# A decoder layer's third phase: values by four full-width products in k's bank, k in one product, attended rows tile by tile

## Chip, core, metric

One NeuronCore of a Trainium2 chip computes the layer. The time is the device time of one execution in microseconds. TensorE multiplies matrices, VectorE, ScalarE and GpSimd work element by element, SyncE starts transfers. TensorE writes its results to PSUM, eight banks of 512 columns of 32-bit numbers in each of 128 partitions; the other engines read them there.

## What is computed

128 sequences of 64 tokens with 128 features pass through linear attention with a lookup activation, then cross attention to a context, then a small mixture of experts, each followed by a layer norm. The change lies in the cross attention, of which the reference keeps this:

```python
q = (x @ WQ).reshape(b, s, H, DK).transpose(0, 2, 1, 3)          # H = 16 heads, DK = 8
k = (encoder_output @ WK).reshape(b, s, H, DK).transpose(0, 2, 1, 3)
v = (encoder_output @ WV).reshape(b, s, H, DK).transpose(0, 2, 1, 3)
scores = jnp.where(m != 0, NEG, jnp.einsum('bhqd,bhkd->bhqk', q, k) / SQRT_DK)
ctx = jnp.einsum('bhqk,bhkd->bqhd', jax.nn.softmax(scores, axis=-1), v).reshape(b, s, d)
return ctx @ WO
```

All matrices are 32-bit numbers. The profile shows each such product as two records.

## The kernel before

Tokens are worked on in tiles of 128, two sequences each, and four tiles form a group; there are 16 groups (NG) and 64 tiles (NT). Phase 1 is the linear attention and phase 2 the lookup activation; both run over groups. Phase 3, from about 255 us to the end, holds cross attention and experts. It is a software pipeline written out by hand: every engine has a function `phase3(s, p)` that lists, in its own order, what it does in stage s, in four slots t = 0 to 3, one for each tile n = 4s + t. Stage s works on scores, softmax and weighing of group s, on the projections of group s + 1, on output product and norm of group s - 1 and on the experts of groups s - 1 and s - 2. Engines meet only in semaphores: `wait_ge` waits for a count, `then_inc` adds to it, and an engine's instructions run in order, so that all behind a wait wait with it. The loops are unrolled, and the order of an engine's work is the order of the text.

TensorE's slot: turn the probabilities of tile n (`turn_probabilities`, L1437), one or two small jobs, open the scores of two later tiles (`scores_open`, L1419, slots 0 and 2), weigh the values of tile n (`weigh_values`, L1449), close the scores (`scores_close`, L1430). Its small jobs are `turn_y` and the four expert products of earlier groups in slot 0, the output product `rows_product(bank(6), attT, w_xo)` (L1244) and q's product (`project_qk`, L1485) in slot 1, the values' product (`project_v`, L1495) in slot 2, three expert products (`moe`, L1507) in slot 3. The product of k for the next group (`project_k_half`, L1487) is in two halves of 256 columns, one in front of the close of slot 0 and one behind it, in bank 5. The close of slot 0 waits for `max_ready`: VectorE must first have taken maxima of the opened half of the scores (`opened_maxima`, L1056).

`project_v` makes 16 products: for each of 8 sequences u and each half h of the features, 64 tokens are the weights and 64 columns of `w_xv` the moving operand, so that even heads land in partitions 0 to 63 and odd heads in 64 to 127 of bank 4. `copy_v` (L786) on ScalarE takes bank 4 into `v2` with two copies of 64 partitions and 512 columns. Bank 4 is also that of y's transposes and of q; k, and two of the expert products, use bank 5 (`MOE_BANK`, L45).

`weigh_values` puts even tiles into the first 144 columns of bank 7 and odd tiles into the next 144. VectorE's `xattend` (L1042) divides the rows of two tiles at once by their sums, a reciprocal (L1048) and a product (L1050): tiles 0 and 1 at the end of slot 1, tiles 2 and 3 in slot 3. Only in the last stage are tiles 2 and 3 taken one by one. VectorE's order in a stage (L1161): small maxima of the experts' gate, opened maxima, shift of tile 2 (L1072, L1089), residual with the output product (L1146) and its statistics, shift of tile 3 (L1076, L1082), `xattend` of tiles 0 and 1, the gate's weights, the mask of the next group (L1157), shift of the next group's tile 0, `xattend` of tiles 2 and 3, shift of its tile 1, last statistics.

## Time and profile before

| | |
|---|---|
| Median of 3 runs | 550.61 us (549.78 to 551.66) |
| The profiled execution, its own time | 552.82 us |
| Its span | 551.1 us |
| TensorE, products | 500.5 us busy, 91% |
| TensorE, weight loads | 375.0 us, 68%, beside the products |
| VectorE | 399.5 us, 72% |
| GpSimd | 373.1 us, 68% |
| ScalarE | 351.3 us, 64% |
| Mean TensorE clock granted | 0.984 of full speed |

Busy shares are means over three phases and say little of one edit. For that, one stage is read in the timeline, row by row: when each instruction starts, how long it runs, and, where its engine stood idle before it, for how long and what released it. A wait for several semaphores is put down to the one that the profile saw last. The ends of products are modelled. "Issue" as a releaser means that the engine waited for nothing that the profile shows.

### The profile page before, as it was taken

The page shows a single profiled execution, that of the slowest core. Times are in us where ns is not written, and L with a number is a line of the kernel's source. Part 1 is how long each engine was busy: PE and PEld are TensorE (multiplying, and loading weights), DVE is VectorE, ACT ScalarE, POOL GpSimd, SP SyncE. Part 2 cuts the span into 40 slices and gives each one's busy share as a digit, 9 for nine tenths or more (in the row PEclk, how much of TensorE's full clock was granted, in tenths as well). Part 3 has the DMA queues.
Part 4 walks back from the last instruction along what each step waited for, and adds up shares of the span by engine and source line. Part 5 has one row for each costly group of instructions (what it writes and reads, how often), then busy time and mean ns, then how long its engine had stood idle before and what let it go on. Part 6 is the DMA issues. An engine that isn't in the chain of part 4 may idle for free. (4 is left out here: it accounts for less than half of the span.)

```text
span 551.1 us, 23040 instructions
## 1 busy us (share of the span) xinstructions
PE 500.5 (91%) x9358; PEld 375.0 (68%) x9358; DVE 399.5 (72%) x1356; ACT 351.3 (64%) x637; POOL 373.1 (68%) x684
## 2 busy tenths in 40 slices
PE   3899999998999999999899999989999999999780
PEld 1677777775777777676667776767767677767570
DVE  3777777765677667756568788878778788887866
ACT  2566666656777777764576677757666677766641
POOL 3666666645668774746156878897878778797734
PEclk9999999999999999999899999999999999999977
DMA  6540000000000000010110210221101110110001
GB/s 169 157 133 2 3 2 1 4 2 1 2 0 2 2 1 1 2 30 3 32 32 4 51 44 12 52 51 51 32 24 51 52 39 24 44 51 23 23 2 58
DMA packets 24747, 17.44 MB, mean 32 GB/s; under 512 B 2113, under 2 KB 22465, under 8 KB 24641
## 3 DMA queue, kind: packets, MB, share of 16 engines
q1 hardware_dynamic: 24208, 15.90, 10.6%
q8 instruction: 74, 1.21, 0.9%
q14 instruction: 33, 0.26, 0.2%
q10 hardware_dynamic: 432, 0.07, 0.1%
HBM read 11.77 MB, written 4.19 MB: 29 GB/s over the span
## 5 line engine op out<-in xcount | busy, mean ns | idle before, releaser
L810 ACT ACTIVATE soft<-pair 128x1024 f32<-128x1024 f32 x64 | 51.9, 810 | 50.1 <-PE pair L1445 49.5
L803 ACT ACTIVATE soft<-soft,row_scale 128x512 f32<-128x512 f32 x96 | 66.2, 721 | 15.4 <-DVE soft L1089 10.4
L1387 PEld LDWEIGHTS pair<-w,gel 128*128 128x128 f32 x512 | 60.5, 192 | 8.2 <-issue 5.9
L1387 PE MATMUL pair<-w,gel 128*128 128x128 f32 x512 | 62.7, 276 | 1.0 <-ACT gel L736 1.0
L1348 PE MATMUL pair<-hT,w 128*128 128x512 f32 x128 | 58.3, 595 | 1.3 <-ACT lev L731 1.3
L553 POOL TENSOR_SCALAR k_exp<-k_sb,quad_mask 128x512 f32<-128x512 f32 x64 | 43.2, 693 | 20.1 <-ACT k_sb L783 10.6
L1445 PE MATMUL pair<-ident,soft 128*128 128x128 f32 x384 | 55.6, 281 | 1.3 <-ACT soft L803 1.3
L1076 DVE TENSOR_REDUCE neg_max<-pair 128x16 f32<-128x512 f32 (+1 forms) x48 | 41.1, 856 | 14.5 <-PE pair L1412 14.4
L1445 PEld LDWEIGHTS pair<-ident,soft 128*128 128x128 f32 x384 | 43.3, 141 | 12.0 <-issue 6.4
L515 POOL TENSOR_TENSOR X<-X,proj_sb 128x512 f32<-128x512 f32 x16 | 20.4, 1274 | 35.3 <-ACT proj_sb L694 35.3
L1412 PE MATMUL pair<-k_exp,qT 32*32 32x128 f32 (+1 forms) x2048 | 43.5, 336 | 0.0
L1089 DVE TENSOR_TENSOR soft<-pair,neg_max 128x512 f32<-128x512 f32 x64 | 41.2, 686 | 1.1
L1348 PEld LDWEIGHTS pair<-hT,w 128*128 128x128 f32 x128 | 22.9, 190 | 24.0 <-issue 23.5
L1239 PE MATMUL pair<-ident,xn 128*128 128x128 f32 x192 | 30.6, 283 | 8.6 <-DVE xn L361 8.6
L321 POOL TENSOR_SCALAR veps_b<-mv_b 128x4 f32<-128x4 f32 (+1 forms) x33 | 7.8, 236 | 44.4 <-DVE mv_b L312 25.8
L736 ACT ACTIVATE gel<-lev 128x512 f32<-128x512 int8 x64 | 36.4, 621 | 0.9 <-DVE lev L985 0.9
L1239 PEld LDWEIGHTS pair<-ident,xn 128*128 128x128 f32 x192 | 23.7, 146 | 18.5 <-issue 15.8
L323 POOL TENSOR_TENSOR rstd_b<-veps_b,minus_half 128x4 f32<-128x4 f32 (+1 forms) x33 | 34.4, 1042 | 2.8
L323 POOL TENSOR_TENSOR rstd<-veps,minus_half 128x4 f32<-128x4 f32 x32 | 33.2, 1039 | 2.7
L1476 PEld LDWEIGHTS pair<-v,soft 128*32 128x32 f32 x2048 | 23.6, 109 | 14.7 <-issue 14.7
L1244 PE MATMUL pair<-w_kv,hT 128*128 128x128 f32 x256 | 33.5, 285 | 0.0
L305 DVE BATCH_NORM_STATS2 stats_b<-X 128x6 f32<-128x128 f32 x128 | 28.0, 281 | 5.7 <-DVE X L1146 2.8
(145 smaller groups left out, 1260.1 us busy)
## 6 DMA issues: line engine op xcount, KB each, us to landing
X<-in_x SPq DMA_DIRECT2D x16, 256.0 KB, 3.2
cT<-in_ctx SPq DMA_DIRECT2D x16, 256.0 KB, 3.9
out_rows<-X SPq DMA_DIRECT2D x15, 256.0 KB, 2.6
mask_rows<-in_mask_early SPq DMA_DIRECT2D x16, 128.0 KB, 3.9
w<-in_L_attn_w SPq DMA_DIRECT2D x2, 256.0 KB, 3.3
out_rows<-X SPq DMA_DIRECT2D x2, 128.0 KB, 1.8
w_kv<-in_L_attn_wk SPq DMA_DIRECT2D x1, 64.0 KB, 2.9
w_kv<-in_L_attn_wv SPq DMA_DIRECT2D x1, 64.0 KB, 2.6
```

The lines of the kernel that those rows point to most:

```text
L323: nc.gpsimd.tensor_tensor(rstd[:, ts], veps[:, ts], minus_half[:, ts], ALU.pow)\
L553: last = nc.gpsimd.tensor_scalar(k_exp[q][:, h, :], k_sb[:, :], quad_mask[:, h:h + 1], 0.0, ALU.mult, ALU.add)
L736: nc.scalar.activation(gel[:, p, f, :], lev[f][:, :], ACT.Gelu_apprx_tanh, scale=QSTEP).then_inc(gel_ready, 1)
L803: nc.scalar.activation(part, part, ACT.Exp, scale=row_scale[:, n:n + 1])\
L810: nc.scalar.activation(pT[par].rearrange("p (a c) -> p a c", a=2), turned, ACT.Copy)\
L1076: nc.vector.tensor_reduce(neg_max[par][:, :].rearrange("p (a h) -> p a h", a=2), scores, AX.X, ALU.max, negate=True).then_inc(max_ready, 1)
L1089: nc.vector.tensor_tensor(rows[:, heads, :], scores[:, half, :, :], neg_max[par][:, heads].unsqueeze(2).broadcast_to([P, HH, S]), ALU.add) ...
L1239: last = nc.tensor.transpose(dst[:, P * t:P * (t + 1)], src[:, t, :], ident[:, :])
L1348: nc.tensor.matmul(bank(up_bank(s, f)), w_1[:, P * f:P * (f + 1)], hT[p][:, :], start=True, stop=True).then_inc(up_done, 1)
L1387: last = nc.tensor.matmul(bank(6 + q)[:, P * t:P * (t + 1)], gel[:, q, f, P * t:P * (t + 1)], w_2[:, f, :], start=(f == 0), stop=(f == NF ...
L1412: last = nc.tensor.matmul(pair[t % 2][b * QW:(b + 1) * QW, quad // 2, heads], qT[p][rows, batch + first:batch + first + QW], k_exp[p][rows ...
L1445: last = nc.tensor.transpose(dst, probability_rows(n)[:, P * i:P * (i + 1)], ident[:, :])
```

## The change

Four things are done. `project_v` makes four products, one for each tile u, of 128 tokens as weights and all 128 columns of `w_xv`, in bank 5 (bank 1 for group 0, as before). Even and odd heads then lie beside each other, and the two sequences of a tile in the two halves of the partitions, so that `copy_v` sorts them with four copies of 64 partitions and 256 columns: sequence b, head parity h. The product of k is made in one piece of 512 columns behind the close of slot 0. `weigh_values` puts every tile into the same 144 columns of bank 7 and waits in each tile until the tile before was attended, and `xattend` takes one tile at a time: tile 0 in slot 0 behind the opened maxima, tile 1 where the pair was, tile 2 in slot 2 behind the next mask, tile 3 in slot 3. Waits follow the banks: `turn_y` waits for the copy of q and no longer for that of the values, the values' product waits for the copy of k, the first expert product for the copy of the values and the third for that of q.

```diff
--- before.py
+++ after.py
@@ -786,12 +786,13 @@
             def copy_v(g, q):
                 after(act, pv_done, g * TG - TG)
                 act.wait_ge(xv_done, g + 1)
-                for h in range(2):
-                    rows = slice(h * S, (h + 1) * S)
-                    last = nc.scalar.activation(
-                        v2[q][rows, :, :, h, 0:DH],
-                        bank(first_bank(g, 4))[rows, :].rearrange("p (b i e) -> p b i e", i=HH, e=DH),
-                        ACT.Copy)
+                values = bank(first_bank(g, 5)).rearrange("p (u h i e) -> p u h i e", u=TG, h=2, e=DH)
+                for b in range(2):
+                    for h in range(2):
+                        batches = v2[q][h * S:(h + 1) * S, :, :, h, 0:DH] \
+                            .rearrange("p (u b) i e -> p u b i e", b=2)
+                        last = nc.scalar.activation(batches[:, :, b, :, :],
+                                                    values[b * S:(b + 1) * S, :, h, :, :], ACT.Copy)
                 last.then_inc(v2_ready, 1)
 
             def probabilities(n):
@@ -1039,19 +1040,16 @@
                     ln_statistics(dve, ln_a, r, lambda t: X[:, r * TG + t, :], stats_b, mv_b,
                                   ln_a.offs, r * 2)
 
-            def xattend(n, p, part):
+            def xattend(n, p, t):
 
                 dve.wait_ge(pv_done, n + 1)
-                count = len(part)
-                src = bank(7)[:, H * HV * (part[0] % 2):H * HV * (part[-1] % 2 + 1)] \
-                    .rearrange("p (h e) -> p h e", e=HV)
-                nc.vector.reciprocal(rec[:, 0, 0:H * count], src[:, :, DH]).then_inc(xrec_ready, count)
+                src = bank(7)[:, 0:H * HV].rearrange("p (h e) -> p h e", e=HV)
+                nc.vector.reciprocal(rec[:, 0, 0:H], src[:, :, DH]).then_inc(xrec_ready, 1)
                 dve.wait_ge(xrec_ready, n + 1)
-                nc.vector.tensor_tensor(
-                    att[p][:, part[0]:part[-1] + 1, :].rearrange("p t (h e) -> p (t h) e", e=DH),
-                    src[:, :, 0:DH],
-                    rec[:, 0, 0:H * count].unsqueeze(2).broadcast_to([P, H * count, DH]),
-                    ALU.mult).then_inc(xatt_ready, count)
+                nc.vector.tensor_tensor(att[p][:, t, :].rearrange("p (h e) -> p h e", e=DH),
+                                        src[:, :, 0:DH],
+                                        rec[:, 0, 0:H].unsqueeze(2).broadcast_to([P, H, DH]),
+                                        ALU.mult).then_inc(xatt_ready, 1)
 
             def opened_maxima(n):
 
@@ -1166,26 +1164,27 @@
                         gate_top(old, p)
                     if t == 0 and exists(s):
                         opened_maxima(n + 2)
+                        after(dve, xatt_xposed, s - 1)
+                        xattend(n, p, t)
                     if t == 1 and exists(s):
                         shift(n + 1, 0)
                     if t == 1 and exists(prev):
                         residual(prev, 6, range(TG))
                     if t == 1 and exists(s):
                         shift(n + 2, 1)
-                        after(dve, xatt_xposed, s - 1)
-                        xattend(n, p, (0, 1))
+                        xattend(n, p, t)
                     if t == 1 and exists(old):
                         gate_weights(old)
                     if t == 2 and exists(s + 1):
                         future_keys(s + 1, q)
-                    if t == 2 and s == LAST:
-                        xattend(n, p, (2,))
+                    if t == 2 and exists(s):
+                        xattend(n, p, t)
                     if t == 3 and exists(s + 1):
                         shift(n + 1, 0)
                     if s == LAST and t == 3:
                         residual(*halves[0][:1], 5, halves[0][1])
                     if t == 3 and exists(s):
-                        xattend(n, p, (3,) if s == LAST else (2, 3))
+                        xattend(n, p, t)
                     if t == 3 and exists(s + 1) and s >= 0:
                         shift(n + 2, 1)
                     if t == 3 and exists(old) and s < LAST:
@@ -1449,23 +1448,20 @@
             def weigh_values(n, t, p):
 
                 pe.wait_ge(pT_ready, n + 1)
-                if n % 2 == 0 or n == NT - 1:
-                    after(pe, xatt_ready, n)
-                first = H * HV * (n % 2)
+                after(pe, xatt_ready, n)
                 if n % 2:
                     pe.wait_ge(v4_ready, (n // TG + 1) * QB)
                     pe.wait_ge(future_ready, n // TG + 1)
                     for b in range(QB):
                         nc.tensor.matmul(
-                            bank(7)[b * QW:(b + 1) * QW, first:first + H * HV],
+                            bank(7)[b * QW:(b + 1) * QW, 0:H * HV],
                             future[p][:, t // 2, b * QW:(b + 1) * QW],
                             v2[p][:, t // 2 * QB + b, :, :, :].rearrange("p i h e -> p (i h e)"),
                             start=True, stop=False)
                     for i in range(QB):
                         for b in range(QB):
                             last = nc.tensor.matmul(
-                                bank(7)[b * QW:(b + 1) * QW,
-                                        first + QB * HV * i:first + QB * HV * (i + 1)],
+                                bank(7)[b * QW:(b + 1) * QW, QB * HV * i:QB * HV * (i + 1)],
                                 pT[1][:, P * i + b * QW:P * i + (b + 1) * QW],
                                 v4[p][:, t // 2 * QB + b, i, :, :].rearrange("p h e -> p (h e)"),
                                 start=False, stop=i == QB - 1)
@@ -1484,10 +1480,6 @@
 
                 nc.tensor.matmul(dst, w[:, :], src[:, :], start=True, stop=True).then_inc(done, 1)
 
-            def project_k_half(q, half):
-                cols = slice(GW // 2 * half, GW // 2 * (half + 1))
-                return nc.tensor.matmul(bank(5)[:, cols], w_xk[:, :], cT[q][:, cols], start=True, stop=True)
-
             def turn_y(g):
                 pe.wait_ge(ln_a.done, g + 1)
                 transposes(X[:, tiles(g), :], bank(first_bank(g, 4)), y_xposed)
@@ -1495,13 +1487,9 @@
             def project_v(g, q):
 
 
-                for u in range(2 * TG):
-                    for h in range(2):
-                        last = nc.tensor.matmul(bank(first_bank(g, 4))[h * S:(h + 1) * S,
-                                                                       FH * u:FH * (u + 1)],
-                                                cT[q][:, S * u:S * (u + 1)],
-                                                w_xv[:, FH * h:FH * (h + 1)],
-                                                start=True, stop=True)
+                for u in range(TG):
+                    last = nc.tensor.matmul(bank(first_bank(g, 5))[:, P * u:P * (u + 1)],
+                                            cT[q][:, P * u:P * (u + 1)], w_xv[:, :], start=True, stop=True)
                 last.then_inc(xv_done, 1)
 
             def moe(g, t):
@@ -1537,7 +1525,7 @@
                         turn_attended(q, 6, range(TG))
                     if t == 0 and exists(g):
                         after(pe, moe_ready, (s - 1) * TG - 1)
-                        after(pe, v2_ready, g)
+                        after(pe, q_ready, g)
                         turn_y(g)
                     if t == 1 and exists(r):
                         pe.wait_ge(xattT_ready, r + 1)
@@ -1546,7 +1534,7 @@
                         pe.wait_ge(yT_ready, g + 1)
                         project_qk(yT, w_xq, bank(4), xq_done)
                     if t == 2 and exists(g):
-                        pe.wait_ge(q_ready, g + 1)
+                        pe.wait_ge(k_ready, g + 1)
                         project_v(g, q)
                     if t == 2 and s == LAST:
                         pe.wait_ge(xatt_ready, n)
@@ -1565,22 +1553,20 @@
                         if n == 0:
                             pe.wait_ge(ysum_ready, NG)
                         weigh_values(n, t, p)
+                    if exists(s) and t % 2 == 0 and n + 2 < NT:
+                        scores_close(n + 2, n + 3)
                     if t == 0 and exists(g):
                         pe.wait_ge(ctx_loaded[q], (g - q) * 8 + 16)
                         after(pe, moe_ready, s * TG - TG)
                         after(pe, k_ready, g)
-                        project_k_half(q, 0)
-                    if exists(s) and t % 2 == 0 and n + 2 < NT:
-                        scores_close(n + 2, n + 3)
-                    if t == 0 and exists(g):
-                        project_k_half(q, 1).then_inc(xk_done, 1)
+                        project_qk(cT[q], w_xk, bank(5), xk_done)
                     if t == 3 and exists(r) and s < LAST:
                         pe.wait_ge(y2T_ready, r + 1)
                         if exists(g):
-                            pe.wait_ge(k_ready, g + 1)
+                            pe.wait_ge(v2_ready, g + 1)
                         for u in range(TG - 1):
                             if u == 2 and exists(g):
-                                pe.wait_ge(v2_ready, g + 1)
+                                pe.wait_ge(q_ready, g + 1)
                             moe(r, u)
```

## Rows read from the trace of the kernel before

**Rows 1.** Windows, phase 3 by stage: us, engines' busy us (records), clock, DMA, GB/s

```profile
289.61:306.71 17.10, 16.52 (x451) 12.28 (x443) 14.07 (x45) 12.01 (x24) 11.70 (x20) 1.00 0.02 4
...
sum 227.29, PE 216.33 PEld 159.67 DVE 182.87 ACT 156.31 POOL 183.35; mean PE 16.64 PEld 12.28 DVE 14.07 ACT 12.02 POOL 14.10
```

**Rows 2.** Timeline, slot 0: start us, us, engine line op out<-in, [idle before <-releaser]

```profile
411.03 0.82 PE L1476 MATMUL pair<-v,soft 128*32 128x18 f32 x64
...
411.35 0.69 DVE L1059 TENSOR_REDUCE neg_max<-pair 128x8 f32<-128x512 f32 x1
...
411.78 0.70 PE L1489 MATMUL pair<-cT,w_xk 128*128 128x256 f32 x2
...
412.41 0.28 PE L1401 MATMUL pair<-causal_bf,quad_ident 32*128 32x256 bf16 x4
...
413.22 0.70 PE L1489 MATMUL pair<-cT,w_xk 128*128 128x256 f32 x2
...
413.53 0.69 DVE L1072 TENSOR_REDUCE neg_max<-pair 128x8 f32<-128x512 f32 x1 [1.49 <-PE pair L1412]
...
413.75 0.60 PE L1445 MATMUL pair<-ident,soft 128*128 128x128 f32 x4
```

**Rows 3.** Timeline, slot 1 of that stage, and the same place 71.8 us earlier

```profile
414.19 1.06 PE L1244 MATMUL pair<-w_xo,attT 128*128 128x128 f32 x8
...
415.08 1.02 PE L1485 MATMUL pair<-yT,w_xq 128*128 128x512 f32 x2
...
415.46 0.68 DVE L1146 TENSOR_TENSOR X<-X,pair 128x512 f32<-128x512 f32 x1
...
416.04 0.45 PE L1459 MATMUL pair<-v,future 128*32 128x144 f32 x8
...
343.74 1.06 PE L1244 MATMUL pair<-w_xo,attT 128*128 128x128 f32 x8
...
344.84 0.69 DVE L1146 TENSOR_TENSOR X<-X,pair 128x512 f32<-128x512 f32 x1
```

**Rows 4.** Timeline, end of VectorE's chain and slot 2 of that stage

```profile
417.74 1.15 PE L1500 MATMUL pair<-w_xv,cT 128*64 128x64 f32 x32
...
418.43 0.69 DVE L1082 TENSOR_TENSOR soft<-pair,neg_max 128x512 f32<-128x512 f32 x1
...
419.22 0.28 PE L1401 MATMUL pair<-causal_bf,quad_ident 32*128 32x256 bf16 x4 [0.33 <-ACT soft L810]
```

**Rows 5.** Timeline, attended rows of two tiles, the weighing and the next shift

```profile
419.04 0.35 DVE L1048 RECIPROCAL rec<-pair 128x32 f32<-128x32 f32 x1
...
419.49 0.42 DVE L1050 TENSOR_TENSOR att<-pair,rec 128x256 f32<-128x256 f32 x1
...
420.06 0.79 PE L1476 MATMUL pair<-v,soft 128*32 128x18 f32 x64
...
421.89 1.23 DVE L1076 TENSOR_REDUCE neg_max<-pair 128x16 f32<-128x1024 f32 x1 [0.28 <-PE pair L1412]
```

**Rows 6.** Timeline, the last stage: its second scores, attended rows of one tile

```profile
516.92 0.28 PE L1401 MATMUL pair<-causal_bf,quad_ident 32*128 32x256 bf16 x4 [0.39 <-DVE neg_max L1059]
...
524.48 0.69 PE L1521 MATMUL pair<-ident,att 128*128 128x128 f32 x2 [2.95 <-DVE att L1050]
...
526.30 0.26 DVE L1048 RECIPROCAL rec<-pair 128x16 f32<-128x16 f32 x1 [0.76 <-PE pair L1476]
...
526.59 0.29 DVE L1050 TENSOR_TENSOR att<-pair,rec 128x128 f32<-128x128 f32 x1
```

**Rows 7.** Timeline of ScalarE: copies of the values, of tile 3, of 256 columns

```profile
419.78 1.26 ACT L791 ACTIVATE v<-pair 64x512 f32<-64x512 f32 x2
...
422.27 0.60 ACT L810 ACTIVATE soft<-pair 128x512 f32<-128x512 f32 x1 [1.23 <-PE pair L1445]
...
525.21 0.39 ACT L827 ACTIVATE attT<-pair 128x256 f32<-128x256 f32 x1 [0.82 <-PE pair L1521]
```

**Rows 8.** Timeline, inside a weighing of values

```profile
368.23 0.24 PE L1476 MATMUL pair<-v,soft 128*32 128x18 f32 x4 [0.94 <-issue]
```

## The prediction

> **What bounds the kernel now.** I read the windows of the decoder's third phase first (the tail of the span from about 255 us on, where everything that the diff touches runs, save the values of group 0). Thirteen full stages, measured from one product of k to the next, take 227.29 us together, 17.5 each; one of the shortest takes 17.10, with TensorE busy 16.52 us in it and 16.64 on the mean [rows 1]. So TensorE is almost always at work, and a stage is 17.1 us plus something irregular. The other engines are at 12 to 14 us of 17.1. That does not say yet that a saving on TensorE is a saving in time: for that the timeline of one stage has to be read for who releases whom.
>
> TensorE's order in a stage has three places where it meets VectorE. At slot 0 it weighs values (411.03), multiplies the first half of k (411.78) and closes the scores (412.41), which must wait for VectorE's early maxima, 411.35 to 412.04 [rows 2]. At slot 1 VectorE takes the scores at 413.53, runs without idle time through the shift of tile 2, the residual at 415.46, the statistics and the shift of tile 3, which ends at 419.12 [rows 2 to 4]. At slot 2 TensorE is done with the values at about 418.9, sits 0.33 us and opens scores at 419.22 [rows 4]. The profile puts that wait down to ScalarE's copy, but the subtraction on VectorE ended at 419.12, 0.10 before, so I take VectorE as the one waited for. From the close of slot 0 to the open of slot 2 the stage is therefore set by VectorE: 419.22 - 413.22 = 6.00 us, and TensorE has 0.33 us to spare there.
>
> **Values by four products.** Thirty-two records of 64 columns took 1.15 us (two records for each of 16 products) [rows 4]. The nearest row for four products of 128 columns with 128 columns of weights is the output product, eight records, 1.06 us, and 0.89 to the start of the next [rows 3]. So 0.1 to 0.25 us less TensorE time, but in a place where TensorE then waits 0.33 us for VectorE: worth nothing in the 15 stages of phase 3, and -0.1 once, for group 0, whose values are multiplied in phase 2 where no such wait follows. The new wait on the copy of k is free: k ended at 413.92, a copy of 128x512 takes 0.60 us, and the values start only at 417.74 [rows 2, 4, 7].
>
> **Four copies for two.** ScalarE took 1.26 us for two of 64x512 [rows 7]. The nearest row for 256 columns is 0.39 us [rows 7], so four take 1.3 (pipelined like the two) to 1.6 us, 0.0 to 0.3 more, at 419.8 to 421.4 instead of 421.04. ScalarE's next work, turned probabilities of tile 3, starts only at 422.27 [rows 7]. Cover of 0.9 us: nothing. The expert products now wait for this copy one product earlier, at about 424, also covered.
>
> **k in one piece after the close.** Before: first half 0.63 us (411.78 to 412.41), second half 0.53 (413.22 to 413.75), 1.16 in all [rows 2]. One product of 512 columns, the one for q, takes 416.04 - 415.08 = 0.96 from its start to the next product [rows 3]. TensorE saves 0.20. But the first half also hid the wait for the maxima. Without it the close waits for VectorE: 412.04 plus the step from VectorE to TensorE, which the last stage shows, since it has no k: there TensorE idles 0.39 us at this very place, released by the maxima [rows 6]. So close moves from 412.41 to about 412.19: 0.22 earlier, with 0.41 of idle time in front. Counted from there: all of k follows, 0.96 instead of 0.53, so the output product starts 0.96 + 0.44 = 1.40 after the close instead of 0.97, and ends 1.06 later, at +2.46. VectorE needs it for the residual. It reaches the residual 415.46 - 413.22 = 2.24 after the close today, and the product ended at 415.25 (2.03), 0.21 ahead. In another stage the product ended at 343.74 + 1.06 = 344.80 and the residual began at 344.84: this is the case where it is waited for, and the step is 0.04 [rows 3]. New: 2.46 + 0.04 = 2.50, that is 0.26 late. Against the 0.22 gained at the close: +0.04 at most, I take +0.02 a stage (the close may come a little earlier still), 15 stages, **+0.3**. TensorE itself gets to the open of slot 2 at +0.96 instead of +0.53 and less the shorter values, 0.2 to 0.3 later than before against the close, and has 0.33: it just fits.
>
> **Attended rows tile by tile.** Each pair costs VectorE 0.80 us (419.04 to the next at about 419.84) [rows 5]; single tiles exist in the last stage, 526.30 to 526.88, 0.58 [rows 6]. Four for two: +0.72 us of VectorE a stage. Where do they lie? Tile 0 goes in front of the shift of tile 2, where VectorE waited 1.4 us; it can start when the values of slot 0 are done, about 412.1, and ends by 412.7, before the scores arrive at 413.3: covered by 0.6. Tile 2 goes in front of the next group's first shift, where VectorE waited 0.28 us [rows 5]; the chain before it is 0.21 shorter, together 0.49 against 0.58: that shift comes 0.1 later. What hangs on it is TensorE's turn of the first probabilities, behind ScalarE's exponentials; the cover there is about 0.2 to 0.3, so 0. At slot 3 the chain is 0.21 shorter again and the delay is made good before the early maxima. TensorE's new waits, one in front of every weighing, are for rows that are done 0.9 us (tile 2), over 2 us (tile 0) before. One is on the path and gets better: at slot 2 TensorE opens scores until about 420.03, and the pair's rows end at 419.91, so that the weighing at 420.06 waits for them by some 0.03 [rows 4, 5]. With one tile they end 0.21 earlier: -0.03 x 15 = **-0.4**. In the last stage TensorE waits 2.95 us for just these rows before it turns them [rows 6]; one tile for two ends that 0.21 earlier: **-0.2**.
>
> **Fewer instructions.** 24 products and their weight loads in two records each for the values, one for k: 48 + 4 = 52 of about 894 records a stage. The stages' irregular part is 227.29 - 13 x 17.10 = 5.0 us. Part of it shows as idle time inside a run of equal products that wait on no semaphore, put down to issue: 0.94 us in front of the last 4 of 64 [rows 8]; there are four such rows in the phase, all at this place. It looks like the sequencer running out of instructions: 64 products and as many loads start within 0.75 us there [rows 2], right behind the stretch that the change thins out. Bounds: 0 (the stalls only move), -5.0 (all gone), and +3 (they fall in worse places, as often as now and as long as the longest). I take an eighth, **-0.6**.
> The Trainium skill ("Runtime: NRT & Kernel Launch", Instruction fetch mechanics) states that instructions are refilled in blocks of 256 while the current block runs, and that this fetch is hidden. By that rule the last term is nothing and the result would be 550.2; the idle time inside a run without semaphores speaks against the rule, though no row shows the fetch that is waited for.
>
> **The sum.** -0.1 + 0.3 - 0.4 - 0.2 - 0.6 = -1.0 us against the profiled execution's 552.82 (span 551.1), 551.8. That execution was 2.2 us above the median of the runs, 550.61, so 549.6.
>
> **The rivals.**
> First, the early close is kept. If the output product does not hold the residual (its record's end is modelled, and the step of 0.04 may be too long), VectorE's 6.00 us start 0.22 earlier and the open of slot 2 follows: -0.22 x 15 = -3.3 where the sum has +0.3, 549.6 - 3.6 = 546.0. For it: VectorE is the bound between the two places. Against: the stage in which residual and product meet at 0.04. I give it 0.13.
> Second, the stalls go: -3 to -5 instead of -0.6, 545.2 to 547.2, the middle 546.2. For it: they lie in the densest stretch, right behind the values. Against: most stages with the same code show nothing there. 0.15.
> Third, slower: the close of slot 0 has lost its cover. Today the maxima may come up to 0.23 late unseen; afterwards every delay of VectorE passes to TensorE, and from there back into VectorE's own chain. The place is 411.35: VectorE ends its small maxima just then and the scores arrive just then. If the added rows of tile 2, or of tile 0 in front of the shift, put VectorE 0.2 late (instead of 0.1 early), each stage grows by 0.2 and the residual's 0.04: +3.4 with the other terms, 553.0. It decides from the point where tile 2's rows delay the next shift by more than the 0.21 given back at slot 3. With stalls that fall in worse places it is of the same size. 0.20.
> Fourth, a V whose products are not shorter, or copies that take 1.6 us: both are covered, the time stays in the forecast's range.
>
> **How the numbers follow.** Forecast 0.52, own range 548.4 to 550.9; first 0.13, second 0.15, third 0.20. A measurement of this kernel can tell about 0.3%, 1.65 us: faster is below 548.96, slower above 552.26. Faster: the first two and 0.09 of the forecast, 0.37. Slower: most of the third, 0.18 (its small end is within). Same: 0.45. The range reaches from the middle of the second rival to the third: 546.0 to 552.9.
>
> **What would show it.** Right: in front of the close of slot 0 idle time of about 0.4 us on TensorE, released by the early maxima, in all stages; the residual waits for the output product by about 0.25; the wait at the open of slot 2 is still there, 0.1 to 0.3; V about 0.9 to 1.0 us; shortest stage 17.05 to 17.15. Rival one: residual without a wait, shortest stage 16.9. Rival two: shortest stage the same, but all near it. Rival three: the idle time at the close above 0.5, or the weighing of slot 3 or 1 behind rows. Wrong altogether: a wait in front of a place that I called covered.

## The result and the profile after

The kernel with the change takes **553.87 us** (median of 13 runs, 552.59 to 556.40); the kernel before, in the same comparison, 551.23 (13 runs, 548.91 to 552.75). The ratio is **1.0047 [1.0025, 1.0069]**: slower by 2.6 us. The prediction was 549.6, with a range of 546.0 to 552.9; the median lies 1.0 above its top. It set out from a median of 550.61 for before, which 13 runs put at 551.23: 0.6 of the 4.3 us between forecast and result come from there.

| | before | after |
|---|---|---|
| Median | 551.23 us | 553.87 us |
| The profiled execution, its own time | 552.82 us | 552.99 us |
| Its span | 551.1 us | 551.2 us |
| TensorE, products | 500.5 us | 494.9 us |
| VectorE | 399.5 us | 407.2 us |
| ScalarE | 351.3 us | 354.9 us |
| Instructions, all engines | 23040 | 22289 |
| Clock granted | 0.984 | 0.984 |

One thing has to be kept in mind for all that follows: the two profiled executions differ by 0.17 us only, because that of before was 1.6 us above its median and that of after 0.9 below. The traces show what the schedule became and where irregular time falls. How much of it an execution has on the mean, only the medians tell.

Four stages of the kernel after, windows from one product of q to the next; columns as in [rows 1]:

```profile
293.64:310.76 17.12, 16.19 (x418) 11.93 (x417) 14.50 (x49) 12.27 (x25) 14.28 (x26) 1.00 0.02 5
380.30:399.03 18.73, 16.61 (x418) 12.05 (x417) 14.59 (x49) 12.28 (x25) 14.24 (x26) 1.00 0.13 38
399.03:416.16 17.13, 16.20 (x419) 12.01 (x418) 14.50 (x49) 12.28 (x25) 14.28 (x26) 1.00 0.14 43
433.28:451.56 18.28, 16.36 (x418) 11.97 (x417) 14.71 (x49) 12.33 (x25) 14.21 (x26) 1.00 0.18 49
```

A clean stage takes 17.12 to 17.13 us where it took 17.10 [rows 1], with 0.33 us less of TensorE work in it. VectorE has four more instructions and 0.43 us more work. Stages of 18 us and more are still there. (A clean stage is one without a stall, at the full clock. A window's record counts take in records that reach over its ends; the program has 442 product records in a stage of before and 416 in one of after.)

The clean stage that begins at 399.03, TensorE's timeline (start us, us, engine line op out<-in, [idle before <-releaser]), to be read against [rows 2 to 5]:

```profile
411.91 0.82 PE L1472 MATMUL pair<-v,soft 128*32 128x18 f32 x64
413.06 0.28 PE L1400 MATMUL pair<-causal_bf,quad_ident 32*128 32x256 bf16 x4 [0.33 <-DVE neg_max L1057]
...
413.86 1.13 PE L1481 MATMUL pair<-cT,w_xk 128*128 128x512 f32 x2
414.83 0.60 PE L1444 MATMUL pair<-ident,soft 128*128 128x128 f32 x4
415.26 1.06 PE L1243 MATMUL pair<-w_xo,attT 128*128 128x128 f32 x8
...
418.72 1.06 PE L1491 MATMUL pair<-w_xv,cT 128*128 128x128 f32 x8
420.13 0.28 PE L1400 MATMUL pair<-causal_bf,quad_ident 32*128 32x256 bf16 x4 [0.35 <-ACT soft L811]
```

The same stage, VectorE's timeline:

```profile
412.22 0.69 DVE L1057 TENSOR_REDUCE neg_max<-pair 128x8 f32<-128x512 f32 x1 [0.30 <-PE pair L1411]
412.86 0.26 DVE L1047 RECIPROCAL rec<-pair 128x16 f32<-128x16 f32 x1
...
414.18 0.69 DVE L1070 TENSOR_REDUCE neg_max<-pair 128x8 f32<-128x512 f32 x1 [0.74 <-PE pair L1411]
...
416.36 0.69 DVE L1144 TENSOR_TENSOR X<-X,pair 128x512 f32<-128x512 f32 x1 [0.17 <-PE pair L1243]
...
419.34 0.69 DVE L1080 TENSOR_TENSOR soft<-pair,neg_max 128x512 f32<-128x512 f32 x1
```

TensorE's waits over the whole trace of after (waited for: us in total, times, longest), and its turn of the attended rows in the last stage, which stood 2.95 us behind them in [rows 6]:

```profile
PE pair L1400 <- DVE neg_max L1057: 5.3, 16, 0.4
```
```profile
524.40 0.69 PE L1509 MATMUL pair<-ident,att 128*128 128x128 f32 x2 [2.64 <-DVE att L1049]
```

The schedule came out as predicted, stage by stage. In front of the close of slot 0 TensorE idles 0.33 us, released by the maxima, in all 16 stages. k follows in one piece, 0.97 us to the next product. The output product ends at 415.26 + 1.06 = 416.32 and holds the residual, which starts at 416.36 after 0.17 us of idle time (0.25 predicted); in the waits of the whole trace VectorE's residual is held by this product 16 times, before only twice. V takes 1.06 us for 1.15 and a wait of 0.35 is still behind it. The places that were called covered show no new wait.

What is left is the idle time put down to issue, in the middle of runs of equal products. In after's trace:

```profile
264.65 0.41 PE L1411 MATMUL pair<-k_exp,qT 32*32 32x128 f32 x4 [0.75 <-issue]
...
384.27 0.28 PE L1400 MATMUL pair<-causal_bf,quad_ident 32*128 32x256 bf16 x4 [0.35 <-ACT soft L811]
384.48 0.66 PE L1411 MATMUL pair<-k_exp,qT 32*32 32x256 f32 x32
385.07 0.82 PE L1472 MATMUL pair<-v,soft 128*32 128x18 f32 x64
385.83 0.28 PE L1400 MATMUL pair<-causal_bf,quad_ident 32*128 32x256 bf16 x4
386.04 0.66 PE L1411 MATMUL pair<-k_exp,qT 32*32 32x256 f32 x24
387.89 0.42 PE L1411 MATMUL pair<-k_exp,qT 32*32 32x128 f32 x8 [1.19 <-issue]
...
441.15 0.27 PE L1444 MATMUL pair<-ident,soft 128*128 128x128 f32 x1 [0.99 <-issue]
457.39 0.28 PE L1400 MATMUL pair<-causal_bf,quad_ident 32*128 32x256 bf16 x4 [0.24 <-issue]
```

Before, four such rows stood at one place, in front of the last 4 of 64 records of slot 2's weighing [rows 8], together 2.66 us. Two more, which the prediction did not count, stand inside the weighing of an odd tile:

```profile
284.00 0.41 PE L1466 MATMUL pair<-v,soft 128*32 128x36 f32 x25 [0.22 <-issue]
...
423.73 0.41 PE L1466 MATMUL pair<-v,soft 128*32 128x36 f32 x25 [0.29 <-issue]
```

Now each of the four is at another place: in front of the last 8 or 4 of 32 records of slot 2's close, just behind that close, in front of a close. Together the stalls are 3.17 us in either trace.

### The profile page after: what moved, and what is told of

It reads as the page before. It is cut to its first block and busy times, and to the rows that moved or that the text cites. A ratio compares the mean times of both kernels' runs of the same rounds, so it can differ in the third digit from the quotient of the medians.

```text
span 551.2 us, 22289 instructions
## 1 busy us (share of the span) xinstructions
PE 494.9 (90%) x8944; PEld 370.3 (67%) x8944; DVE 407.2 (74%) x1418; ACT 354.9 (64%) x669; POOL 372.0 (67%) x684
## 3 DMA queue, kind: packets, MB, share of 16 engines
q8 instruction: 71, 1.16, 0.9%
## 5 line engine op out<-in xcount | busy, mean ns | idle before, releaser
L1411 PE MATMUL pair<-k_exp,qT 32*32 32x128 f32 (+1 forms) x2048 | 44.8, 333 | 1.9 <-issue 1.9
L305 DVE BATCH_NORM_STATS2 stats<-X 128x6 f32<-128x128 f32 x128 | 27.6, 278 | 5.4 <-DMA X<-in_x 4.0
```

Of the source, the lines that this page charges most:

```text
L305: last = nc.vector.bn_stats(stats[:, t, :], rows(t))
L1411: last = nc.tensor.matmul(pair[t % 2][b * QW:(b + 1) * QW, quad // 2, heads], qT[p][rows, batch + first:batch + first + QW], k_exp[p][rows ...
```

## Theories

**A, the instruction blocks.** Count TensorE's instructions in the program: each product record and each load record is one, so a 32-bit product is four and a bf16 product or a transpose two, and each wait that stands as an instruction of its own is one more. The stalls put down to issue in phase 3 then lie at one position of a raster of 256 instructions: counted from the start of the kernel's TensorE program, 84 stalls in the 14 traces of this case stand at position 190 or 191 of 256. (Another 14 idle stretches put down to issue, of 0.16 to 0.24 us, do not: 13 in before_wandering and one in k_one_piece_filled. They lie in front of the open of slot 2 behind tiny products, where TensorE waited for VectorE before.) The stall at 387.89 shows a whole block: the 256 instructions in front of it are 2 x (4 + 32 + 64 + 4 + 24) = 256, that is everything from the open at 384.27 on. The profile's queue of instructions moved 1.16 MB in 71 packets, 16 KB each, and 74 packets in before, whose program has some 800 instructions more. So TensorE's instructions come in blocks, and where a block has been worked off faster than the next one is ready, TensorE waits at the block's end. A stage of before has 896 instructions (442 products, 442 loads, 12 waits), and two stages are exactly 7 blocks: block ends fall in the same places again and again. A stage of after has 846 (48 fewer for V, 4 fewer for k, 2 more waits), and the block ends wander through all places, also those behind the densest instructions.

**B, the schedule.** The time is lost by the edits themselves: k in one piece takes the cover from the close, or V and its copies hold something in executions that the trace didn't catch.

The Trainium skill ("Runtime: NRT & Kernel Launch", Instruction fetch mechanics) gives blocks of 256 instructions, refilled while the current one runs; with that these traces agree. It calls the cost of crossing a block's end "mostly hidden": from 255 us on, 668 block ends in the 14 traces pass without a stall and 84 do not, with 0.16 to 1.76 us each.

## The experiments

**1. The block ends moved, nothing else (pad128_before).** Before, with waits that are already fulfilled ahead of TensorE's first work:

```diff
+            for _ in range(128):
+                pe.wait_ge(const_ready, 1)
             pe.wait_ge(w1_loaded, PHASE1_WEIGHTS)
```

> The kernel before, with 128 extra waits on a count long reached at the very start of TensorE's program, where TensorE is idle anyway. Nothing of the schedule changes; all later TensorE instructions lie half a 256-instruction block further on. Theory A (the change lost time because instructions are refilled in blocks, and the kernel before, whose two stages take exactly seven blocks, had block ends at harmless places): the time moves by 1 us or more from the 551.2 of before, more likely up, to 552 to 554. Theory B (the loss is in the changed schedule itself): within 0.5 us of before, once a later start of the first product is taken off.

Measured: 563.2 us (560.76 to 569.01), ratio **1.0227 [1.0184, 1.027]**. That is far above the 552 to 554 that theory A expected. Of the loss, some 2 us are the waits themselves (the first product comes 2.3 us later); 10 us are not. (The profiled execution, 569.01, is the slowest of the six.) Two waits share an instruction, so the shift was 64, not 128. Two stages in windows, then TensorE's timeline in the second:

```profile
297.70:314.80 17.10, 16.53 (x445) 12.30 (x444) 14.06 (x45) 12.00 (x24) 14.28 (x26) 1.00 0.01 4
314.80:334.80 20.00, 18.45 (x445) 13.49 (x444) 14.30 (x45) 12.50 (x24) 14.23 (x26) 0.91 0.16 41
```
```profile
319.02 0.28 PE L1403 MATMUL pair<-causal_bf,quad_ident 32*128 32x256 bf16 x4 [0.33 <-ACT soft L810]
...
320.79 0.66 PE L1414 MATMUL pair<-k_exp,qT 32*32 32x256 f32 x24
322.67 0.42 PE L1414 MATMUL pair<-k_exp,qT 32*32 32x128 f32 x8 [1.22 <-issue]
...
324.42 0.71 PE L1461 MATMUL pair<-v,future 128*32 128x144 f32 x8
...
325.53 2.31 PE L1510 MATMUL pair<-w_moe,y2T 128*128 128x263 f32 x6
```

The place moved from the last 4 records of the weighing to the last 8 of 32 of the close behind it: 2 x (4 + 4 + 24) = 64 instructions on, and since two stages are 7 blocks, block ends of two neighbouring stages lie 128 apart, so that 64 back and 64 on is the same. The clean stage is untouched, 17.10. Each second stage takes 19.9 to 20.4, the last 18.35. The waits of 0.84 to 1.50 us at this place are 7 in phase 3 (8.6 us in the summary of waits), and behind all but the shortest the clock falls: the granted clock is 0.50, the lower of its two levels, from 323.6 to 327.0 and 1.00 again afterwards, and six records of expert products take 2.31 us at 325.53 where they take 1.60 in an undisturbed stage. In before, the block that ends in the last 4 records of the weighing holds V, the open and 60 records:

```profile
399.77 1.15 PE L1500 MATMUL pair<-w_xv,cT 128*64 128x64 f32 x32
...
403.51 0.24 PE L1476 MATMUL pair<-v,soft 128*32 128x18 f32 x4 [0.66 <-issue]
```

What a stall waits for can be read from the packets of the instruction queue in the traces. In all 14, from 255 us on, there is one packet for each block end. Some ends of blocks (us; "lag" is from the end of the packet to TensorE's first product behind the block's end):

| trace | block begins | its packet | next block begins | stall | lag |
|---|---|---|---|---|---|
| before | 295.58 | 295.40 to 296.52 | 298.46 | none | 1.94 |
| before | 329.95 | 330.43 to 331.33 | 332.83 | none | 1.50 |
| before | 364.23 | 366.05 to 367.02 | 368.23 | 0.94 | 1.21 |
| before | 399.78 | 401.16 to 402.14 | 403.51 | 0.66 | 1.37 |
| pad128_before | 319.02 | 320.11 to 321.47 | 322.67 | 1.22 | 1.20 |
| after | 384.28 | 385.35 to 386.61 | 387.89 | 1.19 | 1.28 |
| after | 411.33 | 411.23 to 412.15 | 413.55 | none | 1.40 |
| shift128_before | 454.23 | 456.62 to 457.59 | 459.05 | 1.76 | 1.47 |

All 84 stalls end 1.19 to 1.61 us (median 1.38) after the block's packet, and at none of the 668 ends without a stall is it shorter than 1.19. So TensorE waits for the next block's instructions. How long depends on two things: how fast the block is worked off, and when its packet starts, which is 0.25 to 4.0 us after the block's beginning where there is a stall. The same block of before (V, the open, 60 records) passes at 298.46 and 332.83 and stalls at 368.23 and 403.51, because its packet started later. This is theory A; theory B has no edit here to act on.

**2 to 4. Each part of the change alone**, in one comparison with run 1.

> The kernel before with k's product in one piece behind the close of slot 0, and nothing else. Theory B puts the loss here: the close waits about 0.4 us for the maxima and the output product holds the residual, 0.04 to 0.17 us a stage, 551.8 to 553.8. Theory A: 4 instructions fewer a stage let the block ends drift slowly, 550.5 to 553.5 with the stalls at other places than before; the shortest stage 17.10 to 17.15.

> The kernel before with the attended rows taken tile by tile in one place of bank 7, and nothing else. TensorE's instructions are the same but for one wait in front of every odd weighing. Both theories expect little: shortest stage 17.05 to 17.10, 550.5 to 551.5. If VectorE's 0.72 us more a stage were what costs, 552 to 554 with TensorE waiting in front of a weighing or of the close.

> The kernel before with the values by four products in k's bank and four copies, and nothing else. 48 instructions a stage fewer. Theory B: covered, 551.0 to 551.3. Theory A: this part carries the loss, since it alone makes the block ends drift through the stage: 552.5 to 554, with a shortest stage of 17.10 as before and stalls put down to issue at places that differ from stage to stage.

```diff
 k_one_piece
-                        project_k_half(q, 0)
                     if exists(s) and t % 2 == 0 and n + 2 < NT:
                         scores_close(n + 2, n + 3)
-                        project_k_half(q, 1).then_inc(xk_done, 1)
+                        project_qk(cT[q], w_xk, bank(5), xk_done)
 rows_one_tile: xattend(n, p, t) for each tile, as in the change
 v_four_products: project_v and copy_v of the change, in bank 5
```

| | instructions a stage | ratio | clean stage |
|---|---|---|---|
| before | 896 | 1 | 17.10 |
| k_one_piece | 892 | 1.0066 [1.0044, 1.0089] | 17.12 to 17.13 |
| rows_one_tile | 898 | 0.9986 [0.9968, 1.0004] | 17.09 |
| v_four_products | 848 | 1.0077 [1.0048, 1.0105] | 17.04 to 17.10 |

k_one_piece (554.18) and v_four_products (555.50) lie above what either theory expected, 553.8 and 554 at most; rows_one_tile (550.43) is just below the expected 550.5. The parts do not add up: +3.6, -0.8 and +4.2 us are 7.0 where the change costs 2.6. V alone makes the clean stage no longer and is the slowest of all; theory B has no place for that. rows_one_tile has two instructions more than before, both waits, and its block end walks back by two records in every second stage:

```profile
368.16 0.30 PE L1471 MATMUL pair<-v,soft 128*32 128x18 f32 x11 [0.63 <-issue]
...
403.18 0.31 PE L1471 MATMUL pair<-v,soft 128*32 128x18 f32 x13 [0.66 <-issue]
...
437.92 0.32 PE L1471 MATMUL pair<-v,soft 128*32 128x18 f32 x15 [0.37 <-issue]
...
472.65 0.32 PE L1471 MATMUL pair<-v,soft 128*32 128x18 f32 x17 [0.39 <-issue]
```

Two instructions a stage are four in two stages, the length of two products with their loads: 11, 13, 15, 17. That is the raster, read off a timeline.

**5 to 7. Other shifts.** Tiny products of two columns into columns of bank 7 that nothing uses, ahead of TensorE's first work, four instructions each:

```diff
+            pe.wait_ge(const_ready, 1)
+            def filler(count):
+                for _ in range(count):
+                    nc.tensor.matmul(bank(7)[0:QW, 500:502], ident[0:QW, 0:QW], ident[0:QW, 0:2],
+                                     start=True, stop=True)
+            filler(32)    # 28 in shift112_before; 42 in shift168_after
```

> The kernel before with 32 tiny products (128 TensorE instructions) ahead of its first one, in TensorE's idle start. Since two stages take exactly 7 blocks of 256 instructions, a shift by half a block only makes odd and even stages change places. Theory A (time is lost where a block ends inside dense instructions, and how much depends on the place): the same as before, 550.5 to 552, against 563.2 for the shift by 64. If a filled start as such costs time, or a shift as such: 555 or more. Shortest stage 17.1 under either.

> The same with a shift by 112. Theory A, from the places at which blocks end (a block is never worked off in less than about 3.65 us, the dense ones would take 2.1 to 3.4): block ends move 16 instructions further down, out of the close of slot 0's end, summed shortfall 7.9 us instead of 10.5 and none above 1 us in a stage: 548.5 to 551. Theory B (the place does not matter below the one bad case): 551.2 as before.

> The changed kernel with a shift by 168 instructions in the idle start. Its stages take 846 instructions, so that block ends wander through the stage and no shift avoids the dense places; with this one two ends instead of four fall where the shortfall is above 1 us. Theory A: 550 to 552.5, 1.5 to 4 us less than the 553.9 of the changed kernel. Theory B (the changed schedule costs the time): 553.5 to 554.5, unchanged.

Measured: shift128_before 554.98 us, 1.0051 [1.0027, 1.0076], and shift112_before 554.11 us, 1.0039 [1.0015, 1.0064]: both slower than theory A expected. shift168_after 551.99 us, 1.0013 [0.999, 1.0035], is where theory A had it, but this shows little alone: the same comparison's before is 552.36, and the interval meets that of after, 1.0025 to 1.0069. The shift by 128 puts the stalls where they were, in front of the last 4 of 64, as expected, but they are longer:

```profile
352.39 0.24 PE L1483 MATMUL pair<-v,soft 128*32 128x18 f32 x4 [1.21 <-issue]
...
459.05 0.24 PE L1483 MATMUL pair<-v,soft 128*32 128x18 f32 x4 [1.76 <-issue]
```

So the place says where TensorE may wait, not how long. At this place the packet starts 1.10 to 2.39 us after the block's beginning in the six stalls of shift128_before, and 2.39 in front of the 1.76; before it is -0.17 to 1.82. Nor is there a shortest time for a block, which the expectation of shift112_before put at 3.65 us: the one of after at 411.33 passes in 2.22 us without a stall, since its packet was early. Shifts that differ by little can't be ranked by place alone.

**8. The stage of after filled up to 896 (after_full_stage)**, with 50 instructions, 12 tiny products and one small transpose, ahead of the close of slot 0 and ahead of V (and 13 tiny products at the start, not shown):

```diff
+                        filler(6, 5)     # ahead of the close of slot 0: 24 instructions
 ...
+                        filler(6, 5)     # ahead of V, with the transpose: 26 instructions
+                        nc.tensor.transpose(bank(5)[0:QW, 304:304 + QW], ident[0:QW, 0:QW], ident[0:QW, 0:QW])
```

> The changed kernel with its 50 missing instructions a stage put back as tiny products where TensorE waits for VectorE anyway (26 ahead of the values' product, 24 ahead of the close of slot 0), and 52 at the start, so that stages take 896 instructions again and blocks end at the same places of the weighing of slot 2 as in the kernel before. Schedule and waits are those of the changed kernel. Theory A: 550 to 551.5, the loss against before gone. Theory B: 553.5 to 555.

Measured: 562.57 us, 1.0196 [1.0161, 1.0231], where 550 to 551.5 was expected. The fillers themselves cost time: on one place of 32 columns they are not short (12 records, 0.47 us to the next product), and seven of the eight stalls stand in the close behind them.

```profile
418.97 0.54 PE L1237 MATMUL pair<-ident 32*32 32x2 f32 x12
...
421.26 0.42 PE L1418 MATMUL pair<-k_exp,qT 32*32 32x128 f32 x9 [0.95 <-issue]
```

The clean stage was 17.56, 0.44 longer than that of after, 6.6 us in 15 stages. Nothing follows for the change.

**9 to 11. The number of instructions alone.** Fillers spread over the four column groups, in each stage ahead of V only, into columns that V then overwrites or nothing reads (after_filled has 13 more at the start, not shown):

```diff
+                for i in range(count):
+                    rows = slice(i % QB * QW, (i % QB + 1) * QW)
+                    nc.tensor.matmul(bank(b)[rows, 500:502], ident[:, rows], ident[:, 0:2],
+                                     start=True, stop=True)
 ...
+                        filler(12, 5)   # after_filled: 846 + 48 + 2 (the small transpose of run 8) = 896
+                        filler(1, 4)    # k_one_piece_filled: 892 + 4 = 896
+                        filler(3, 4)    # before_wandering: 896 + 12 = 908
                         project_v(g, q)
```

> The changed kernel with its 50 missing instructions a stage put back as 12 tiny products and one small transpose ahead of the values' product, spread over four column groups so that they take about 0.3 us and fit into the wait for VectorE at the open of slot 2, and 52 at the start. Stages take 896 instructions again, and blocks end at the same places of the weighings as in the kernel before (3 instructions off). Theory A (place of block ends): the loss goes, ratio to before 0.998 to 1.001 instead of 1.0047, shortest stage 17.12. Theory B (the changed schedule costs the time): 1.004 to 1.006. If the filling itself does not fit, the shortest stage shows it, above 17.2.

> k in one piece as in the run with that part alone (ratio 1.0066), plus one tiny product (4 instructions) a stage ahead of the values' product: 896 instructions a stage again, block ends at the same places of the weighings as before. Theory A: ratio 0.999 to 1.002. Theory B: 1.006 to 1.007, since one more product cannot make it faster.

> The kernel before with three tiny products (12 instructions) a stage ahead of the values' product, where TensorE has 0.33 us to spare; nothing else. Stages take 908 instructions, so that block ends wander as they do in the changed kernel. Theory A: three stages get a shortfall of 1.2 to 1.5 us and the slow clock with it, ratio 1.003 to 1.009, shortest stage 17.1. Theory B: ratio 1.000 to 1.001.

| | instructions a stage | ratio | clean stage |
|---|---|---|---|
| after | 846 | 1.0047 [1.0025, 1.0069] | 17.12 |
| after_filled | 896 | 1.0013 [0.9997, 1.0029] | 17.32 to 17.33 |
| k_one_piece | 892 | 1.0066 [1.0044, 1.0089] | 17.12 |
| k_one_piece_filled | 896 | 1.0017 [1.0001, 1.0032] | 17.12 |
| before_wandering | 908 | 1.0081 [1.0056, 1.0107] | 17.09 |

Each ratio is to the before of its own comparison; the two filled kernels and before_wandering share one. This settles it. Four instructions in a stage, one tiny product, take k_one_piece from +3.6 us to +0.9, with the same schedule. Twelve instructions more in before, which leave its clean stage at 17.09, cost 4.1 us on the median (555.07 against 550.96). And after with 50 more instructions, which lengthen each clean stage by 0.2 us, 3 us in all (the filling was expected to fit, at 17.12), is still faster than without them, 1.0013 against 1.0047, though the two intervals touch. In k_one_piece_filled the stalls are back at one place, in before_wandering they are anywhere:

```profile
401.99 0.24 PE L1482 MATMUL pair<-v,soft 128*32 128x18 f32 x4 [0.77 <-issue]
...
437.46 0.24 PE L1482 MATMUL pair<-v,soft 128*32 128x18 f32 x4 [0.74 <-issue]
...
473.12 0.24 PE L1482 MATMUL pair<-v,soft 128*32 128x18 f32 x4 [0.75 <-issue]
```
```profile
316.49 0.66 PE L1451 MATMUL pair<-ident,soft 128*128 128x128 f32 x4 [0.95 <-issue]
...
351.63 0.44 PE L1418 MATMUL pair<-k_exp,qT 32*32 32x128 f32 x12 [0.89 <-issue]
...
456.80 0.31 PE L1482 MATMUL pair<-v,soft 128*32 128x18 f32 x12 [0.92 <-issue]
```

The stalls at block ends in phase 3 add up to 3.17 us in before, 2.84 in k_one_piece_filled, 5.55 in before_wandering, 6.49 in shift128_before, 9.78 in pad128_before, and 0.85 in after_filled (the two rows below). But each is one execution, and small differences do not follow the medians: k_one_piece has 2.39 and v_four_products 3.68, and the profiled execution of k_one_piece is only 0.4 us above that of before, where the medians are 3.2 apart. The longest stall of before_wandering is 0.95 us, not the expected 1.2 to 1.5, and the clock falls behind one.

```profile
402.98 0.25 PE L1479 MATMUL pair<-v,soft 128*32 128x18 f32 x6 [0.55 <-issue]
...
434.75 0.37 PE L1239 MATMUL pair<-ident 128*32 128x2 f32 x24
...
438.13 0.25 PE L1479 MATMUL pair<-v,soft 128*32 128x18 f32 x6 [0.30 <-issue]
```

**12. A version meant to beat both (reordered).** k_one_piece_filled, with the output product and k moved to the head of slot 1, y's transposes moved between the weighing and the close of slot 0, VectorE's opened maxima ahead of the gate's small ones, and ScalarE's copy of y behind the exponentials of tile 1. Of TensorE's part:

```diff
+                    if t == 1 and exists(r):
+                        rows_product(bank(6), attT, w_xo[:, :]).then_inc(xproj_done, 1)
+                    if t == 1 and exists(g):
 ...
+                        project_qk(cT[q], w_xk, bank(5), xk_done)
                     if exists(s):
                         turn_probabilities(n, t)
```

> A version meant to beat both, built on the kernel before: y's transposes take the place of k's first half ahead of the close of slot 0, the output product and then all of k come right behind that close, VectorE takes the opened maxima before the gate's small maxima, ScalarE copies y after the exponentials of tile 1, and one tiny product a stage keeps 896 instructions. The wait of 0.33 us at the open of slot 2 is used up by k. Expected: shortest stage 16.75 to 16.9 instead of 17.1, 546 to 549 in all, less what block ends at new places cost (up to +3).

Measured: 551.6 us, 1.001 [0.9994, 1.0025], where 546 to 549 was expected. The shortest stage is 17.14. At slot 0 the copy of the turned probabilities is now waited for, since y's transposes no longer cover it, and from the output product (413.17) to the open of slot 2 (419.40) TensorE needs 6.23 us without a wait, more than the 6.00 of VectorE that the move was to shorten:

```profile
410.22 0.28 PE L1407 MATMUL pair<-causal_bf,quad_ident 32*128 32x256 bf16 x4 [0.23 <-ACT soft L810]
...
413.17 1.16 PE L1250 MATMUL pair<-w_xo,attT 128*128 128x128 f32 x8
...
419.40 0.28 PE L1407 MATMUL pair<-causal_bf,quad_ident 32*128 32x256 bf16 x4
```

No kernel here beats before by more than can be told; rows_one_tile, 0.9986 [0.9968, 1.0004], comes nearest.

## Why the prediction was wrong

**What bounds the kernel**: right. VectorE from the close of slot 0 to the open of slot 2, TensorE everywhere else; the wait at that open stayed, 0.35 for 0.33.

**V and its copies**: right. 1.06 us against the 1.15 of before, nothing gained in the stages, since the wait behind it takes it in; no wait for the copies. For group 0 the values take 0.89 us to the next product where they took 1.08, but the first scores of the phase open at 240.75 as they did at 240.69: the 0.1 does not show. V alone left the clean stage at 17.04 to 17.10.

**k in one piece**: right in each step. Idle 0.33 for about 0.4 at the close; the residual held by the output product and starting 0.04 behind its end; +0.02 a stage predicted, and k_one_piece's clean stage is 0.02 to 0.03 longer. With the block ends left in place (k_one_piece_filled) it costs 0.9 us, with an interval from 0.1 to 1.8; 0.3 was predicted.

**Attended rows**: right. Predicted -0.4 and -0.2; the wait in the last stage went from 2.95 to 2.64, and the part alone gave -0.8, with an interval that takes in 0.

**The first rival** did not happen (the residual waits), **nor the second**, as far as the change goes: the stalls did not go, they add up to the same 3.17 us in the trace. Its neighbour, stalls that go where the stage stays at 896 and V's block is filled, is after_filled. **The third** gave the right side and nearly the size, 553.0, by luck, since its mechanism is not what happened: the opened maxima wait 0.30 us for TensorE at 412.22, so VectorE isn't late there. What came true is the sentence beside it, stalls that fall in worse places.

**The step that failed is the term "Fewer instructions".** It took the stalls for a sequencer that runs dry behind dense stretches, asked how much its neighbourhood thins out, and put -0.6 between -5.0 and +3. What the runs showed in its place: the stalls stand at the ends of blocks of 256 instructions, the number of instructions in a stage decides where these ends fall, and this term is most of the +2.6 us. It should have asked where the stalls come from. The evidence was in [rows 8]: four stalls in front of the same 4 of 64 records, in four successive second stages, which points to something periodic that two stages' length happens to be a multiple of. (The prediction read these as all there are; the two others, in the odd weighing, stand at the same position of the blocks.) The count of 52 of about 894 records came near the program's 50 of 896 instructions, and 896 is 3.5 times 256: that gives the raster, and with it that the change breaks it. Then the bound +3 is the likely value: the schedule's terms (+0.3 to +0.5 for 15 clean stages, -0.3 in the last stage) come to about nothing. The size by itself is shown for k: +3.6 us with 892 instructions, +0.9 with 896. That it is the stalls that cost the change its 2.6 us, and not something else in those executions, is inferred from runs 1 and 9 to 11, which change only the count or the place; the profiled execution of after had no more stalls than that of before.

**Open**: why a block's packet starts at once in one stage and over 2 us after the block's beginning in another, which makes stalls at one place last 0.39 to 1.76 us, and why it starts later in shift128_before. Data transfers beside it give no clear rule.

## What to carry to other kernels

When an edit changes the number of instructions of an unrolled stage on an engine that issues them densely (here 256 in some 3 us), count the stage against blocks of 256 before and after, waits included: here a difference of 4 in 892 was worth 2.7 us, as much as the whole change. A tuned kernel may owe part of its time to such an alignment, and an edit can then be judged only with the count restored. Idle time put down to issue that always stands in front of the same record is the sign to look for, and the packets of the instruction queue are the proof.

## What the runs showed of the hardware

- TensorE can wait at the ends of blocks of 256 of its instructions, wherever they fall in the work: 84 stalls in 14 traces, all at one position of 256. One packet of 16 KB comes for each block (74 in before, 71 in after), and TensorE goes on no sooner than 1.19 us after it has ended.
- A block's packet takes 0.9 to 2.0 us (14 traces, from 255 us on). It starts from 1.5 us before the block's first product to 4.0 us after it, and this decides whether a dense block stalls: the same block passes in 2.88 us in before at 329.95 and takes 4.00 at 364.23.
- The clock can fall behind a long stall: behind 1.22 us at 322.67, the granted clock was 0.50 (the lower of its two levels) from 323.6 to 327.0 and 1.00 again afterwards. pad128_before has seven such stretches in phase 3, and full stages with one take 19.9 to 20.4 us, of which the stall is 1.1 to 1.5. Behind the 1.19 of after at 387.89 there is none, and before has one at 267.6 with no stall ahead of it.
- Two waits of TensorE that stand one behind the other share one instruction: 128 of them moved the block ends by 64.
- Products of two columns cost very different times: 12 records on one place of 32 columns 0.47 us to the next instruction, 24 records spread over four places 0.30.
